# Latent attention: queries and keys projected once a batch for all heads, with high and low rows going through DRAM

## What is computed

```
x = x + 0.5 * ffn(layernorm(x))
x = x + attn(layernorm(x), W_dq, W_uq, W_dkv, W_uk, W_uv, W_o)
x = x + 0.5 * ffn(layernorm(x))
```

```
c_kv = x @ W_dkv.T
q = (x @ W_dq.T @ W_uq.T).reshape(B, T, nh, hs)
q_lat = einsum('bqhd,hdl->bhql', q, k_eff)
attn = softmax(causal(einsum('bhql,bkl->bhqk', q_lat, c_kv) / sqrt(hs)))
y = einsum('bhql,hld->bqhd', einsum('bhqk,bkl->bhql', attn, c_kv), v_eff)
```

## Time and profile before

| | |
|---|---|
| median of three runs | 2125.99 us |
| profiled execution, its own time | 2119.46 us |
| its span | 2117.6 us |
| PE busy in the span | 1765.7 us (83%) |
| DVE, ACT, POOL busy | 1332.1, 945.8, 982.2 us |
| attention phase: first statistics on DVE to its last add on POOL | 856.7 to 1301.2 us |

### The profile page before, as it was taken

One profiled execution on the slowest core, in us unless ns is written; L12 is line 12 of the kernel. 1 busy time (PEld: TensorE's weight loads), 2 busy tenths in 40 slices (PEclk: granted clock), 3 DMA queues, 4 the chain that ended last, 5 costly groups with the idle time before them and its releaser, 6 DMA issues. The chain is left out here.

```text
span 2117.6 us, 48273 instructions
## 1 busy us (share of the span) xinstructions
PE 1765.7 (83%) x19914; PEld 1023.4 (48%) x19914; DVE 1332.1 (63%) x2002; ACT 945.8 (45%) x1503; POOL 982.2 (46%) x692
## 2 busy tenths in 40 slices
PE   1578888899988887799999996678888998988886
PEld 1244445555545454455555553344545555555543
DVE  2567777666776663466666664577766676666763
ACT  1234444545455443255555554234444454544542
POOL 2444544455454451544444441444445555545540
PEclk9789999999999999599999998789999999999998
DMA  4334434454444551000000000243444534455541
GB/s 145 38 59 69 71 67 64 78 78 83 69 74 71 78 87 33 12 1 1 1 2 1 2 1 1 38 74 64 65 78 72 87 64 69 73 84 82 93 75 41
DMA packets 66060, 118.94 MB, mean 56 GB/s; under 512 B 13183, under 2 KB 23603, under 8 KB 63667
## 3 DMA queue, kind: packets, MB, share of 16 engines
q1 hardware_dynamic: 65843, 115.85, 32.6%
HBM read 49.61 MB, written 3.28 MB: 25 GB/s over the span
## 5 line engine op out<-in xcount | busy, mean ns | idle before, releaser
L953 POOL TENSOR_TENSOR QK<-QK,RB 128x1024 f32<-128x1024 f32 x128 | 302.6, 2365 | 438.7 <-DMA RB<-RN 438.4
L793 DVE SCALAR_TENSOR_TENSOR TP<-banks,cols,tab 128x1024 f32<-128x1024 f32 x256 | 321.1, 1276 | 89.7 <-PE banks L457 73.6
L947 POOL TENSOR_TENSOR QK<-TP 128x512 f32<-128x512 f32 x128 | 164.6, 1286 | 275.8 <-DVE TP L793 199.3
L1315 DVE TENSOR_REDUCE NM<-banks 128x2 f32<-128x1024 f32 (+3 forms) x256 | 202.9, 820 | 126.4 <-PE banks L1128 126.3
L1244 ACT ACTIVATE PTL<-banks 128x1024 f32<-128x1024 f32 (+1 forms) x192 | 167.9, 883 | 189.0 <-PE banks L1159 186.4
L649 ACT ACTIVATE SQ<-banks 128x512 f32<-128x512 f32 x128 | 76.5, 597 | 281.1 <-PE banks L457 281.1
L816 DVE TRANSPOSE_TENSOR_REDUCE MX<-banks 128x16 f32<-128x512 f32 x256 | 160.4, 683 | 60.1 <-PE banks L494 60.1
L834 DVE TENSOR_TENSOR OT<-banks,OT 128x512 f32<-128x512 f32 x128 | 85.3, 688 | 163.2 <-DMA OT<-sums_d 146.4
L457 PE MATMUL banks<-HTH,wqkv_h 128*128 128x512 f32 x256 | 128.8, 503 | 58.4 <-POOL HTL L939 33.3
L948 POOL TENSOR_TENSOR QK<-TP 128x512 f32<-128x512 f32 x128 | 165.1, 1290 | 0.0
L677 ACT ACTIVATE PT<-banks 128x512 f32<-128x512 f32 x256 | 132.2, 603 | 49.8 <-PE banks L508 49.8
(11 more groups left out here) (182 smaller groups left out, 3667.3 us busy)
## 6 DMA issues: line engine op xcount, KB each, us to landing
RB<-RN SPq DMA_DIRECT2D x512, 64.0 KB, 4.0
OT<-sums_d SPq DMA_DIRECT2D x128, 256.0 KB, 4.0
V<-V SPq DMA_DIRECT2D x32, 512.0 KB, 6.1
V<-V SPq DMA_DIRECT2D x32, 384.0 KB, 7.1
RB<-vars_d SPq DMA_DIRECT2D x32, 256.0 KB, 3.3
X<-in_L_attn_x SPq DMA_DIRECT2D x8, 256.0 KB, 4.5
out<-X SPq DMA_DIRECT2D x8, 256.0 KB, 4.7
wqkv_raw<-in_L_ffn_wqkv SPq DMA_DIRECT2D x1, 1536.0 KB
```

What stands on the lines that cost most here:

```text
L793: nc.vector.scalar_tensor_tensor(out=TP[:, o:o + 2, :], in0=BK[4 + z][:, :].unsqueeze(1).to_broadcast([P, 2, T]), scalar=q, in1=tab[:, e, ...
L947: nc.gpsimd.tensor_tensor(QK[:, m, 0, :], TP[:, 2, :], TP[:, 1, :], ALU.subtract)
L953: nc.gpsimd.tensor_tensor(QK[:, m, :, :], QK[:, m, :, :], RB[:, m, :].unsqueeze(1).to_broadcast([P, 2, T]), ALU.mult).then_inc(S["nr_ok"], 1)
L1315: last = nc.vector.tensor_reduce(NM[:, G % 2, i, 24 + 32 * h0:57 + 32 * h0:32], PAIR[at(m) % RING][:, :, o:o + (i + 1) * P], AX_X, ALU.max ...
```

## The change

Weights are no longer stacked: `fold` holds three plain 128 x 128 matrices, and one projection of a whole batch's queries and one of its keys replace the four of each. ACT takes the high part from the bank (HIGH, `high_q`, `high_k`), DVE the low part (LOW, `low_rows`), and SP writes them into a DRAM tensor laid out by head, row group, number and token: six transfers a batch of 256 KB (`put_rows`), and at the start four that fill the last 8 rows of both buffers with 0 and 1 (the tile LAST). After the six have landed, SP reads each group's queries and its keys back with one transfer of 256 KB each (`get_rows`) into QS and KS, as soon as their slots are free. POOL keeps only the root and the add of the result.

```
@@ constants of mla_phase
-                AHEAD, QRING, KRING = 2, 3, 4
-                C_AT, Q_AT, K_AT = 1, 2, 4
-                XT_AT, XL_AT, V_AT, VL_AT = (AHEAD, 0), (AHEAD, 1), (AHEAD, 5), (AHEAD + 1, 0)
+                QRING, KRING = 3, 4
+                C_AT = 1
+                XT_AT, XL_AT, Q_AT, K_AT, V_AT = (1, 2), (1, 3), (1, 4), (1, 5), (2, 0)
+                QL_AT, KL_AT, VL_AT = (1, 5), (2, 0), (2, 1)
@@ SP
+                        def put_rows(b, s, r, src):
+                            sp.dma_start(rows_d[b % 2, s, :, r, :, :], src).then_inc(S["row_out"], 16)
+                        def get_rows(dst, G, s, slot, arrived):
+                            b, g = divmod(G, GROUPS)
+                            sp.dma_start(dst[:, slot, :], rows_d[b % 2, s, g * LG:(g + 1) * LG, :, :, :]
+                                         .rearrange("h r d t -> (h r d) t")).then_inc(arrived[slot], 16)
...
+                            if G % GROUPS == 0:
+                                sp.wait_ge(S["ql_ok"], b + 1)
...
+                                put_rows(b, 0, 0, HIGH[:, 0, b % 2, :])
+                                put_rows(b, 0, 1, HIGH[:, 0, b % 2, :])
+                                put_rows(b, 0, 2, LOW[:, 0, b % 2, :])
+                                sp.wait_ge(S["kl_ok"], b + 1)
+                                put_rows(b, 1, 0, HIGH[:, 1, b % 2, :])
+                                put_rows(b, 1, 1, LOW[:, 1, b % 2, :])
+                                put_rows(b, 1, 2, HIGH[:, 1, b % 2, :])
+                                sp.wait_ge(S["row_out"], 64 + 96 * (b + 1))
+                            if G >= QRING:
+                                sp.wait_ge(S["qc_ok"], G - QRING + 1)
+                            get_rows(QS, G, 0, G % QRING, qs_in)
+                            if G >= KRING:
+                                sp.wait_ge(S["t_in"], UN * (G - KRING + 1))
+                            get_rows(KS, G, 1, G % KRING, ks_in)
@@ PE
-                        for G in range(AHEAD):
-                            queries(G)
-                            keys(G)
+                        queries(0)
+                        keys(0)
...
+                            claim(B_PREP, ready, b + 1)
...
+                        def queries(b):
+                            project(b, 0, "ql_ok").then_inc(S["q_in"], 1)
+                        def keys(b):
+                            project(b, 1, "kl_ok").then_inc(S["k_in"], 1)
...
-                            if r == Q_AT and G + AHEAD < ALLG:
-                                queries(G + AHEAD)
-                            if r == K_AT and G + AHEAD < ALLG:
-                                keys(G + AHEAD)
@@ ACT
-                            nc.scalar.activation(RAW[:, 0, :], BK[B_PREP][:, :], ACT.Copy).then_inc(S["rq_ok"], 1)
+                            nc.scalar.activation(HIGH[:, 0, b % 2, :].bitcast(F32R), BK[B_PREP][:, :],
+                                                 ACT.Copy).then_inc(S["qh_ok"], 1)
@@ DVE
+                        def low_rows(b, s, high, low):
+                            dve.wait_ge(S[high], b + 1)
+                            nc.vector.tensor_tensor(LOW[:, s, b % 2, :].bitcast(F32R), BK[B_PREP][:, :],
+                                                    HIGH[:, s, b % 2, :], ALU.subtract).then_inc(S[low], 1)
@@ POOL
-                            link(nc.gpsimd.tensor_scalar(HI[:, 0, :].bitcast(F32R), RAW[:, 0, :], low_q, None, ALU.mult))
...
-                            nc.gpsimd.tensor_tensor(QS[:, G % QRING, :].bitcast(F32R), RAW[:, 0, :], HI[:, 0, :],
-                                                    ALU.subtract).then_inc(S["qs_ok"], 1)
```

More of the change, by code:

```diff
@@ L49, in shape_constants @@
     causal = np.where(np.arange(P)[None, :] <= np.arange(P)[:, None], 0.0, BIG).astype(np.float32)
-    part = row % 32 // DG
-    split = [part == 2, part == 1, row % 32 == 24]
+    one = [row % DG == 0]
     hsum = row // 32 == np.arange(32)[None, :] // 8
@@ L55, in shape_constants @@
     place = row % 16 == np.arange(16)[None, :]
-    return np.concatenate([rope, band, causal, causal.T, np.eye(P)] + split + [hsum, cent, pick, place], 1).astype(np.float32)
+    return np.concatenate([rope, band, causal, causal.T, np.eye(P)] + one + [hsum, cent, pick, place], 1).astype(np.float32)
 def macaron(nc, x, W_dq, W_uq, W_dkv, W_uk, W_uv, W_o, wqkv, q_scale, k_scale, wo, ln_g, ln_b,
@@ L142, in macaron @@
             selc = sb("selc", [4 * 16, LG + 16])
[L143 to L146, removed]
+            fold = sb("fold", [P, 3, P])
             b1raw = sb("b1raw", [HC, 3, 2 * DEPTH])
@@ L1041, in mla_phase @@
                 XTL = sb("XTL", [P, 2, T])
-                RAW = sb("RAW", [P, 2, T])
-                HI = sb("HI", [P, 2, T])
+                HIGH = sb("HIGH", [P, 2, 2, T])
+                LOW = sb("LOW", [P, 2, 2, T])
+                LAST = sb("LAST", [P, 2, T])
                 QS = sb("QS", [P, QRING, T])
@@ new lines, in _ @@
+                        sp.wait_ge(S["rows_ok"], 1)
+                        for e in range(2):
+                            put_rows(e, 0, 3, LAST[:, 0, :])
+                            put_rows(e, 1, 3, LAST[:, 1, :])
+                        for G in range(ALLG):
+                            b = G // GROUPS
+                            if G % GROUPS == 0:
+                                sp.wait_ge(S["ql_ok"], b + 1)
+                                if b >= 2:
+                                    for n in range(GROUPS * (b - 1) - GROUPS, GROUPS * (b - 1)):
+                                        sp.wait_ge(qs_in[n % QRING], 16 * (n // QRING + 1))
+                                        sp.wait_ge(ks_in[n % KRING], 16 * (n // KRING + 1))
+                                put_rows(b, 0, 0, HIGH[:, 0, b % 2, :])
[12 more added lines that the diff above has]
+                            get_rows(KS, G, 1, G % KRING, ks_in)
@@ L1260, in _ @@
                         act.wait_ge(S["fold_in"], 16)
-                        nc.scalar.activation(fold_h[:, :, :, :].bitcast(F32R), Wqk_s, ACT.Copy).then_inc(S["fh_ok"], 1)
+                        nc.scalar.activation(fold_h[:, :, :].bitcast(F32R), fold[:, 0:2, :], ACT.Copy).then_inc(S["fh_ok"], 1)
                         high_x(0)
-                        for G in range(AHEAD):
-                            raw_q(G)
-                            raw_k(G)
+                        high_q(0)
+                        high_k(0)
                         values(0)
```

169 lines of the change are left out of this document (73 added, 96 removed).

## The result

The changed kernel is slower: the ratio of its time to that of the kernel before, on the same chip, is 1.0113, 95% interval [1.0081, 1.0144], some 24 us. Its 15 runs spread from 2132.22 to 2196.33 us (median 2169.55) where those of the kernel before stay within 16 us (2117.2 to 2133.37, median 2124.78). I read the change in a second profile of the same kernel, e7_change_again, whose own time is 2139.75 us. Against the profiled execution of before, 2119.46, that is 20.3 more.

What follows compares the result with a forecast made beforehand. PE was taken to bound the kernel. Terms -45.3 - 2.6 - 0.3 + 11.2 + 24 + 14 + 3.5 = +4.5 on 2119.46 gave 2124; with the runs' median 6.5 higher, forecast 2130 us, range 2107 to 2155 (8 in 10).

Steps and rivals of the forecast that it cites:

- setup and first ffn phase: first U: Setup: plain weights copied instead of stacked and no zeros set, -0.3 us, an estimate between 0 and -1.
- start: first projection to first scores: Start of attention: rows must land in DRAM and be read back before the first scores, +3.5 us (+2 to +11).
- first scores to first QC (half clock, two projections gone): First two groups, at half clock: four projections removed, some 0.65 us more saved on each, -2.6 us.
- first to last QC, clock left out: Main loop: -45.3 us for projections removed, +11.2 for batch projections added, +24 for new waits.
- clock at the seams: PE's clock falls at each of 7 batch preparations, 2.0 us each, +14 us (0 to +34).
- The projections that went: Main loop: 30 groups lose both projections at 1.51 us each, -45.3 us; plain groups 10.5 us apart.
- The waits: Batch preparation: PE waits 0.9, 2.2, 2.65 and 0.5 us, 6.2 replacing 2.8 a batch, +24 us over 7.
- the upper bound of 34: Clock term's upper end: the clock stays low for a whole group each time, 4.9 us each, +34 us.
- Rival 3: Clock stays low behind each batch preparation until `attend` of the next group has run: 34 instead of 14, 2150 us; 22%.
- Rival 1: Waits at batch preparation grow no more than they did, so +24 and +14 fall away: 2092 us; 10%.
- Rival 4: Rows come too late, PE waits for SP's transfers at group 0 of each batch: 2165 at 5 us a batch; 3%.

Runs made afterwards that it cites:

- e7_change_again: The changed kernel once more, unchanged, against the kernel before: 2140.1 us median of 7, ratio 1.0082.
- e1_filled: The changed kernel with 9 unread matmuls ahead of the keys and 11 ahead of the values, where PE waits for LOW: 2116.7 us, ratio 0.9923.
- e3_spread: The changed kernel with queries, keys and values projected three steps or more apart, HIGH still behind the exponential: 2080.4 us, ratio 0.9763.
- e5_close_filled: e4_before_close with seven unread matmuls in front of each group's keys, where PE waited: 2145.37 us, ratio 1.0089.
- e8_behind: The changed kernel with 11 unread matmuls directly behind the values, both long waits left bare: 2149.41 us, ratio 1.0113.
- e4_before_close: The kernel before the change, with keys projected one step behind queries in every group: 2299.0 us, ratio 1.0791.
- e10_spread_late: e3_spread with POOL's three MEMSETs moved behind the first batch's four normalized tiles U: 2082.04 us, ratio 0.9802.

## Why the prediction was right, and where not

By the ratio the changed kernel stands at 2125.99 x 1.0113 = 2150 us. That lies in the range of 2107 to 2155, 20 above the forecast of 2130. The forecast's verdict, no change, had 42% and was wrong; slower had 34%. By the plain median, 2169.55, it would lie outside; that it lies inside hangs on how the runs are counted, and on two errors of opposite sign, a clock that cost twice the forecast and an interval without it that came out 4.3 lower. That is luck. Term by term, from e7_change_again and the earlier trace rows:

| part | forecast | measured |
|---|---|---|
| setup and first ffn phase: first U | -0.3 | +0.9 |
| start: first projection to first scores | +3.5 | +2.5 |
| start: U beside the MEMSETs | 0 | +3.8 |
| first scores to first QC (half clock, two projections gone) | -2.6 | -1.1 |
| first to last QC, clock left out | -10.1 | -14.4 |
| clock at the seams | +14 | +28.8 |
| after the last QC | 0 | -0.2 |
| sum | +4.5 | +20.3 |

The line without clock is seven batches of 19.28 + 10.49 + 10.49 + 10.63 and three last intervals, 31.1 together: 387.3 us, against 401.7 before (887.39 to 1289.11); its forecast is -45.3 + 11.2 + 24. The clock is the rest of the 416.1 (893.47 to 1309.56). Two things must be taken along with these two lines. The 401.7 of before holds some 3.6 us of half clock of its own: its first batch takes 55.88 us from QC to QC, the others 52.2. Against that the changed kernel's intervals without clock are 10.8 shorter, nearly the 10.1 forecast. And of the 28.8, 5.6 lie in the first batch, at the half clock of the start; the six falls behind it cost 23.2.

- **The projections that went.** Right: plain groups are 10.48 to 10.50 apart (10.63 the last of a batch), as the one plain period of before, 10.48, had said.
- **The waits.** Right in place and cause at all three uses of the bank. Forecast 0.9, 2.2, 2.65 and 0.5, measured 0.70, 1.98, 2.42 and (for ACT's copy of the values, in e1_filled) 0.3 us: 5.4 instead of 6.2. The seam had been worked out as 9.2 above a plain group, and is 8.8 at most.
- **The clock: the term that was mis-sized.** The step that failed is "3.5 us at half rate cost at most 1.75; with the second wait inside some, 2.0 each". It took one fall from the ffn phase as the pattern. Measured, it is 23.2 / 6 = 3.9 for each fall in e7_change_again, and 54 / 6 = 9.0 in the first profile (461.1 us from first to last QC, 73.8 for the clock, 20 of it in the first batch). The same rows held the warning that I had put at the upper end only: at 900 to 905 PE was fully busy and still at 0.50. For the first profile the upper bound of 34 was too low as well. The Trainium skill, TensorE: Matmul & The Clock Gate, HAM oscillation, was cited for a loss that comes back with each round; the trace agrees, with a fall at each of the six seams that began at full clock.
- **Rival 3** (the clock stays low a group behind each seam, 2150) gave the right size but not by its own sign: it needed 0.50 in the scores of (2,1) in more than half of the seams, and e7_change_again has two of seven, the first profile three. The clock stays low for longer than forecast at every seam, for groups at some.
- **Rival 1** (the waits don't grow) is refuted by the rows of PE, and e3_spread shows what it would have been worth: 2080, lower than the 2092 given for it; the old waits of 2.8 a batch go too.
- **Rival 4 and the transfers.** PE waited for none in the steady phase. The landing in DRAM took 3.0 us where 2.8 was assumed, and reading back 2.7 and 3.0 instead of 4.0; the term is +2.5 where +3.5 was forecast. By the Trainium skill, DMA: Bandwidth & Descriptors, Anatomy of one DMA, each landing was an estimate of 2.6 and the term +1.9; the page gives its figures for transfers that GpSimd issues, these are issued by SyncE, and they took 0.1 to 0.4 longer.
- **Missed.** That POOL, with less to do ahead of them, makes its MEMSETs earlier, beside DVE's U. The prediction put this at nothing, without a reason; it is +3.8. I followed what the change does to PE's order and not what POOL does with the time it gets.

Where did the expected gain go? From first to last QC e3_spread takes 360.7 us, e7_change_again 416.1. Of these 55.4, the waits are 7 x (8.8 - 3.7) = 36, the clock the other 20 (28.8, less the 9.0 that e3_spread loses to it itself, half of them at the start). The removal of 30 groups' projections was worth what it should be; its placing gave it back and more.

## What to carry to other kernels

When work that was spread over groups is gathered into one, look at the buffer it goes through: three uses of one bank in three steps each pay the full round by the other engines, and three steps of distance pay nothing. On PE, price a wait that comes back every round at its length plus the clock behind it, taking as bounds the longest stretch that the trace shows at half rate with PE busy, and if the wait can't be moved, try unread matmuls in it: in e5_close_filled they took back all of the clock's price, in e1_filled most of it. When an engine loses work, see which of its remaining instructions move forward, and beside what.

## What the runs showed of the hardware

- The granted clock of TensorE fell to 0.50 around waits of 2.0 and 2.4 us at six of six seams that began at full clock (e7_change_again), and stayed there while PE was busy with the work of scores again: 7 to 17 us there, waits included, up to 76 us in the first profile. Eleven matmuls of 128 rows in a block ended it at all seven seams of e8_behind. It also fell where PE waited no longer than 0.7 us, twice in e1_filled and once in e3_spread, and held in the kernel before through waits of 1.35 us once a batch. So long waits make it fall more often and are not the whole cause; what is, and what sets the length, stays open.
- A gap of 1.6 us per group left bare gives 2299.0 us, filled 2145.4 (e4_before_close, e5_close_filled), 7%.
- DVE's TENSOR_SCALAR and COPY between tiles in SBUF stood still beside POOL's MEMSET: 4.92 instead of 1.12 us, and 3.55 instead of 0.36, each ending 0.3 to 0.7 us after the last MEMSET (866.91 against 866.63 in e10_spread_late). TENSOR_TENSOR with one operand from a bank took its usual 0.69, and so did one with both operands in SBUF, XTL in the kernel before (863.43, beside POOL's MEMSET of NM from 863.48 to 864.44). The Trainium skill, SBUF — State Buffer, Who interferes with whom, says the same: a copy or tensor_scalar may use the port pair that it shares with GpSimd, one of the two holds it for its whole instruction and the other is blocked; the trace agrees, at this one place.
